# Graph-attention layer on 8192 nodes: the order of the first loads and of the first eight strips

## What is computed

```
in_fts = context @ W_common.T
left   = in_fts @ w_left + b_left
right  = in_fts @ w_right + b_right
logits = left[:, None] + right[None, :]
logits = where(logits >= 0, logits, 0.2 * logits)
logits = where(adj <= 0, -inf, logits)
y      = relu(softmax(logits, axis=-1) @ x)
out    = layernorm(x + y)
```

## Time and profile before

| | us |
|---|---|
| median of 3 runs | 1482.67 (1479.48 to 1483.78) |
| the profiled execution | 1482.25, of which its span 1480.4 |
| PE busy | 1375.9 (93% of the span) |
| DVE busy | 1306.0 (88%) |
| ACT busy | 643.1 (43%) |
| granted TensorE clock, mean | 0.965 |

### The profile page before, as it was taken

The page is one execution under the profiler, slowest core; times in us unless marked ns, Lnnn a source line. Parts: engine busy times, 40 slices in busy tenths (PEclk is TensorE's granted clock), DMA queues, the critical chain, the costliest instruction groups (busy, mean ns, idle before and its releaser), DMA issues.

```text
span 1480.4 us, 28323 instructions
## 1 busy us (share of the span) xinstructions
PE 1375.9 (93%) x12334; PEld 1207.8 (82%) x12334; DVE 1306.0 (88%) x1156; ACT 643.1 (43%) x675; POOL 72.6 (5%) x207
## 2 busy tenths in 40 slices
PE   1038999999999999999999999999999999999998
PEld 0014888888888888888888888888888888888887
DVE  6879999898989989898999989898998989899981
ACT  0187444444434444444435444444444444344441
POOL 0003000000000000000000000000000000000000
PEclk7558999999999999999999999999999999999999
DMA  9995998889899898989899898898989898988860
GB/s 378 314 283 127 232 235 226 228 213 230 221 229 233 217 225 214 238 207 242 217 231 223 215 234 215 225 224 234 229 214 232 207 238 213 236 221 220 208 169 9
DMA packets 82448, 329.59 MB, mean 223 GB/s; under 512 B 19728, under 2 KB 36112, under 8 KB 48528
## 3 DMA queue, kind: packets, MB, share of 16 engines
q1 hardware_dynamic: 79728, 321.47, 84.6%
q10 hardware_dynamic: 2592, 6.29, 1.4%
HBM read 319.29 MB, written 8.39 MB: 221 GB/s over the span
## 4 chain that ended last, share of the span: by engine, by line
PE 89%; SPq 5%; DVE 3%; ACT 2%; DMA 1%; issue 0%; POOL 0%; POOLq 0%; DVEq 0%
PE ps L351 30%; PE ps L354 29%; PE ps L353 29%; SPq L212 3%; DMA T<-in_x_dram 1%; DVE strip L671 1%; ACT X L399 1%; DVE T L715 1%; SPq L207 1%; SPq L235 1%; DVE X L620 0%; ACT X L394 0%; PE pt L325 0%; DVE xs L507 0%; ACT strip L428 0%
## 5 line engine op out<-in xcount | busy, mean ns | idle before, releaser
L351 PE MATMUL ps<-X,T 128*128 128x257 f16 x4096 | 1123.2, 274 | 7.1 <-ACT X L399 4.8
L354 PE MATMUL ps<-X,T 128*128 128x257 f16 x4096 | 1122.8, 274 | 0.0
L353 PE MATMUL ps<-X,T 128*128 128x257 f16 x4032 | 1101.3, 273 | 0.0
L428 ACT ACTIVATE strip<-strip 128x2048 f32<-128x2048 f32 x256 | 489.0, 1911 | 499.5 <-DMA strip<-in_adj_dram 490.1
L671 DVE SCALAR_TENSOR_TENSOR strip<-tab,arow,strip 128x2048 f32<-128x2048 f32 x256 | 598.0, 2336 | 56.8 <-ACT strip L428 56.0
L715 DVE STREAM_TRANSPOSE T<-strip 128x2048 f32<-128x2048 f32 x256 | 589.7, 2304 | 59.3 <-PE ps L354 59.2
L351 PEld LDWEIGHTS ps<-X,T 128*128 128x128 f16 x4096 | 403.0, 98 | 70.4 <-ACT X L399 15.5
L354 PEld LDWEIGHTS ps<-X,T 128*128 128x128 f16 x4096 | 402.5, 98 | 50.1
L353 PEld LDWEIGHTS ps<-X,T 128*128 128x128 f16 x4032 | 394.7, 98 | 48.9
L409 ACT ACTIVATE xs<-ps,small 128x256 f32<-128x256 f32 x64 | 30.4, 474 | 142.4 <-DVE small L720 142.4
L306 POOL TENSOR_SCALAR small<-small 128x1 f32<-128x1 f32 x64 | 12.3, 191 | 1270.5 <-ACT xs L417 1270.5
(11 more groups left out here) (90 smaller groups left out, 214.8 us busy)
## 6 DMA issues: line engine op xcount, KB each, us to landing
strip<-in_adj_dram SPq DMA_DIRECT2D x1016, 256.0 KB, 4.7
xs<-in_L_gnn_context_dram SPq DMA_DIRECT2D x14, 1024.0 KB, 9.9
T<-in_L_gnn_context_dram SPq DMA_DIRECT2D x4, 2048.0 KB, 17.6
X<-in_L_gnn_context_dram SPq DMA_DIRECT2D x4, 2048.0 KB, 34.1
xs<-in_x_dram SPq DMA_DIRECT2D x64, 128.0 KB, 5.2
out_dram<-xs SPq DMA_DIRECT2D x64, 128.0 KB, 5.1
gw<-in_L_gnn_context_dram SPq DMA_DIRECT2D x2, 1024.0 KB, 20.5
xs<-in_x_dram SPq DMA_DIRECT2D x4, 512.0 KB, 36.7
```

Of the source, the lines that this page charges most:

```text
L351: nc.tensor.matmul(ps[o][:, 0:D + 1], hi, X16[:, jb, 0:D + 1], start=(i == 0), stop=False)
L353: nc.tensor.matmul(ps[o][:, 0:D + 1], hi, X16[:, jb, XL:XL + D + 1], start=False, stop=False)
L354: m = nc.tensor.matmul(ps[o][:, 0:D + 1], lo, X16[:, jb, 0:D + 1], start=False, stop=(g > 0 and i == JB - 1))
L428: nc.scalar.activation(s, s, ACT.Relu, scale=KEEP).then_inc(s_m, 1)
```

## The change

Five edits, all to the order of the first eight strips.

1. Only strips 0 and 1 are loaded ahead of `x`; strips 2 and 3 are loaded behind it, on both queues.
2. ACT: `keep(0)` and `keep(1)` come first, then the issues of the last three chunks of `x` with the square sums of a chunk between them, then the issues for strips 2 and 3, then the last two chunks' square sums. `keep(2)` and `keep(3)` now come behind the high parts: 32 high parts, `keep(2)`, 6, `keep(3)`, 6, `keep(4)`, 7, `keep(5)`, 7, `keep(6)`, 6, `keep(7)`.
3. DVE: masks and transposes strips 0 and 1, makes `Fx`, makes 32 low parts, masks and transposes strips 2 to 7, and makes the other 20 low parts behind strip 7.
4. The order of the blocks is 63 to 32, 11 to 0, 31 to 12; POOL starts after 32 low parts.
5. PE: group 0 as 32 blocks' high products, their low products, the other high products and POOL's twelve low ones; then, once strip 7 is transposed, 20 whole blocks of group 1; then the last 20 low products of group 0; then the rest of group 1. Products and their number are the same.

```diff
+    NE = 2
-        order = list(range(JB - 1, -1, -1))
+        order = list(range(JB - 1, HB - 1, -1)) + list(range(NPL - 1, -1, -1)) + list(range(HB - 1, NPL - 1, -1))
+        PL = HB + NPL
+        R1 = 20
-        cut = [0, 44, JB - NPL, JB]
+        cut = [0, HB, HB + 6, HB + 12, HB + 19, HB + 26, JB]
...
             sp.wait_ge(s_v, 2)
-            for n in range(NB):
+            for n in range(NE):
                 for q in (0, 1):
                     strip_quarter(sp, n, q)
             sp.wait_ge(s_dot, 2 * CT)
             for c in range(NX):
                 for q in (0, 1):
                     x_quarter(sp, c, q)
+            for n in range(NE, NB):
+                for q in (0, 1):
+                    strip_quarter(sp, n, q)
...
-            pool.wait_ge(s_xl, JB - NPL)
+            pool.wait_ge(s_xl, HB)
...
+            pe.wait_ge(s_t, SG)
+            for i in range(HB):
+                high_products(0, i, i == 0)
+            for i in range(HB):
+                low_product(0, i)
+            for i in range(HB, JB):
+                high_products(0, i)
+            for i in range(HB, PL):
+                low_product(0, i)
+            pe.wait_ge(s_t, 2 * SG)
+            for i in range(R1):
+                high_products(1, i, i == 0)
+                low_product(1, i)
+            for i in range(PL, JB):
+                m = low_product(0, i, i == JB - 1)
+            m.then_inc(s_mm, 1)
+            for i in range(R1, JB):
+                high_products(1, i)
+                m = low_product(1, i, i == JB - 1)
+            m.then_inc(s_mm, 1)
...
-                rest_of_x(1)
-                rest_of_x(2)
                 keep(0)
                 keep(1)
-                rest_of_x(3)
-                rest_of_x(4)
-                keep(2)
-                keep(3)
-                for c in range(NX):
+                for c in range(2, NX):
+                    rest_of_x(c)
+                    square_sums(c - 2)
+                rest_of_first_group()
+                for c in range(NX - 2, NX):
                     square_sums(c)
-                for n in range(NB, NS):
+                for n in range(NE, NS):
...
-                    if n < SG - 1:
+                    if n + 1 < NE:
                         masked(n + 1)
-                    if n == SG:
+                    if n == NE:
                         x_factors()
                         dve.wait_ge(s_Fx, 1)
-                        for j in order[cut[0]:cut[1]]:
+                        for j in order[0:HB]:
                             low_part(j)
                         masked(n)
-                        for j in order[cut[1]:cut[2]]:
+                        dve.wait_ge(s_xl, HB)
+                    transposed(n, n % NB, g, g % 2, k)
+                    if n == 2 * SG - 1:
+                        for j in order[PL:JB]:
                             low_part(j)
                         dve.wait_ge(s_xl, JB - NPL)
-                    transposed(n, n % NB, g, g % 2, k)
-                    if SG <= n < 2 * SG:
+                    if NE <= n < 2 * SG:
                         masked(n + 1)
```

More of the change, by code:

```diff
@@ L341, in _, with high_products, low_product @@
             pe.wait_ge(s_one_col, 2)
-            for g in range(NG):
+            def high_products(g, i, first=False):
+                jb = order[i]
+                pe.wait_ge(s_xh, i + 1)
+                nc.tensor.matmul(ps[g][:, 0:D + 1], T16[:, g, jb, :, 1], X16[:, jb, 0:D + 1], start=first, stop=False)
+                nc.tensor.matmul(ps[g][:, 0:D + 1], T16[:, g, jb, :, 0], X16[:, jb, 0:D + 1], start=False, stop=False)
+            def low_product(g, i, last=False):
+                jb = order[i]
+                if HB <= i < PL:
+                    pe.wait_ge(s_xp, NPL - jb)
+                else:
+                    pe.wait_ge(s_xl, lows[i] + 1)
+                return nc.tensor.matmul(ps[g][:, 0:D + 1], T16[:, g, jb, :, 1], X16[:, jb, XL:XL + D + 1], start=False,
+                                        stop=last)
@@ L343, in _ @@
+            m.then_inc(s_mm, 1)
[3 more added lines that the diff above has]
+            m.then_inc(s_mm, 1)
+            for g in range(2, NG):
                 o = g % 2
                 pe.wait_ge(s_t, (g + 1) * SG)
-                if g >= 2:
-                    pe.wait_ge(s_y, g - 1)
-                for i, jb in enumerate(order if g == 0 else range(JB)):
+                pe.wait_ge(s_y, g - 1)
+                for jb in range(JB):
@@ L348, in _ @@
                     hi, lo = T16[:, o, jb, :, 1], T16[:, o, jb, :, 0]
[L349 to L355, removed]
@@ L356, in _ @@
-                    if i == JB // 4 and g % LB == 2 and g // LB + 1 < NLB:
-                        spread_left(g // LB + 1)
[L358 to L365, removed]
+                    nc.tensor.matmul(ps[o][:, 0:D + 1], hi, X16[:, jb, 0:D + 1], start=(jb == 0), stop=False)
@@ L366, in _ @@
+                    nc.tensor.matmul(ps[o][:, 0:D + 1], hi, X16[:, jb, XL:XL + D + 1], start=False, stop=False)
+                    m = nc.tensor.matmul(ps[o][:, 0:D + 1], lo, X16[:, jb, 0:D + 1], start=False, stop=(jb == JB - 1))
+                    if jb == JB // 4 and g % LB == 2 and g // LB + 1 < NLB:
+                        spread_left(g // LB + 1)
                 m.then_inc(s_mm, 1)
@@ L373, in _ @@
             act.wait_ge(s_v, 2)
-            for n in range(NB):
+            for n in range(NE):
                 for q in (2, 3):
                     strip_quarter(nc.scalar, n, q)
-            for c in range(1):
+            for c in range(2):
                 for q in (2, 3):
@@ L389, in rest_of_x, with rest_of_first_group @@
                     x_quarter(nc.scalar, c, q)
+            def rest_of_first_group():
+                for n in range(NE, NB):
+                    for q in (2, 3):
+                        strip_quarter(nc.scalar, n, q)
             def square_sums(c):
@@ L476, in _ @@
             with act.Else():
-                for c in range(1, NX):
+                for c in range(2, NX):
                     rest_of_x(c)
+                rest_of_first_group()
                 for c in range(NX):
@@ L775, in _ @@
                 dve.wait_ge(s_Fx, 1)
-                for j in order[0:JB - NPL]:
+                for j in order[0:HB] + order[PL:JB]:
                     low_part(j)
```

5 lines of the change are left out of this document (3 added, 2 removed).

## The result

The changed kernel takes 1484.73 us (median of 19 runs) beside 1480.69 for the kernel before (20 runs): a ratio of 1.0024, with a 95% interval of 1.0016 to 1.0031. A twentieth run of the changed kernel, at a granted clock of 0.55 where the others had 0.96, took 2503 us and is left out here and in all comparisons. The difference is 3.6 us by the ratio and 4.0 by the medians, slower by less than the 0.3% that I called no change. The forecast was +3.4 us.

The account below looks back on a forecast made before the run. Up to group 2 the load of x, then DVE's work behind the scale factors, were taken as the bound; PE after. Group 2 later, +1.3, plus clock, +2.1, gave +3.4 us, 1486.0; 8-in-10 range 1482.5 to 1489.5.

Parts of the forecast that it names:

- x earlier: Load of x: two strips, 2.1 MB, no longer ahead of it, so it lands 8.0 us earlier, bounds 6.0 and 9.0.
- A: The moment ACT starts its first high part: 98.44 us in the profile before, forecast 90.4 after the change.
- the 88 that I had set as the limit: Sign on the load of x: the forecast is wrong if x lands before 83 or after 88 us.
- DVE's extra work: DVE masks and transposes strips 2 and 3 behind the scale factors, 4.58 us a strip, 9.2 us more.
- The steps from A: DVE's path from ACT's first high part to strip 11's transposition: group 2 starts 73.5 us behind, at 163.9, +1.3 us.
- The thin cover of ACT's masks: Strips 2 to 7: ACT's masks stay 0.4 to 0.9 us ahead of DVE; each 0.1 us short costs that much.
- The clock: PE idles 4.4 us before group 2, then runs at half clock: +2.1 us, bounds 1.3 and 2.8.
- A (overtaking, +7.3): Rival: strips 2 and 3 on SP's queue overtake ACT's last quarters of x, which gains only about 4 us; chance 0.12.
- B: Rival: DVE is held by a late mask or group 0's products ending late, 1 to 3 us, 1487 to 1489; chance 0.10.
- C: Rival: PE's 4.4 us of idleness cost nothing or little, 1483.9 to 1484.5; chance 0.13.
- D: Rival: DVE's path is shorter than read, group 2 starts when PE allows, without idle, -3.2 us, 1479.5; chance 0.05.
- step 4: PE in groups 0 and 1: its later start is covered, group 1 being done 4.4 us ahead of strip 11.

Follow-up runs that it names:

- SP waits: The changed kernel, but SP issues its quarters of strips 2 and 3 only once the last chunk of x has landed; 1484.15 us, ratio 1.0026.
- both wait: The changed kernel with SP's strips 2 and 3 held until x has landed and ACT's issued behind its last square sum; 1483.77 us, ratio 1.0013.
- issues first: The changed kernel, but ACT issues all its x and strips 2 and 3 ahead of its first mask, square sums behind; 1486.52 us, ratio 1.0043.
- fed gap: The changed kernel with 36 extra matmuls, their results overwritten, on PE between groups 1 and 2; 1483.40 us, ratio 1.0013.
- groups in turn: The changed kernel without PE's interleaving: group 0 is finished before group 1 starts; 1483.60 us, ratio 1.002.
- 24 on POOL: The changed kernel with POOL making 24 low parts instead of 12 and PE finishing group 0 before group 1; 1477.84 us, ratio 0.9983.

## Why the prediction was right

The time was forecast as +3.4 us and came as +3.6 to 4.0; the mechanism was DVE's longer path against the earlier x, with a clock loss, and the profile shows each.

1. **x earlier** is the term that was mis-sized: 8.0 us forecast, 6.2 in the profiled pair (A at 92.27, not 90.4; the last square sum at 87.73, just inside the 88 that I had set as the limit). That is near the lower bound of 6.0, the bytes at x's own rate. The step priced x as a whole, and its upper bound took the two queues to run evenly. They did not: SP's last quarter of x landed at 82.3, 11.6 us earlier than before, ACT's at 87.7, only 2.0 earlier than the 89.7 of the lines below, and the later one counts. (An even end would have been near 85, an estimate from these landings, and would have gained 8.9 us.) The slow end of x, 232 GB/s from 80 to 90 us after 365 in the middle, is not new: the kernel before has 278 and 238 from 86 to 96. How much of ACT's delay is overtaking by SP's strips and how much its later issue stays open; holding the strips won back 0.1 to 1.6 us in timed runs. Nor is 6.2 firm: where the loads are the same, A is 91.18 to 92.80 in four profiles, and 98.44 and 98.97 in two with the order of before, a gain of 5.6 to 7.8; and if DVE's 9.3 and the clock's 1.7 hold in the timed runs, their +3.6 to 4.0 leaves 7.0 to 7.4 for it.

ACT's last quarter of x in the kernel before:

```profile
L212 ACTq DMA_DIRECT2D T<-in_x_dram x1: 4106/4106/4106, 71.2 to 71.2; - x1
DMA to landing us min/median/max: 18.5/18.5/18.5
```

2. **DVE's extra work**: 9.2 us forecast; group 2 moved from A+64.2 to A+73.5, 9.3.
3. **The steps from A** held to 0.2 us: first matmul of PE at A+24.15 (24.0), strip 7 transposed at A+42.4 (42.2), 20 low parts in 7.96 us (8.1), group 2 at A+73.47 (73.5). The three kernels that change only x's part (SP waits, both wait, issues first) have A+73.48 or A+73.49. The thin cover of ACT's masks held.
4. **PE**: done with group 1 at A+69.0 (69), idle 4.5 us (4.4). Strip 8's transposition was not held (its cover was put at 1.0 us).
5. **The clock**: 2.1 forecast, 1.7 in the profile, between the bounds of 1.3 and 2.8; shown by the fed gap, which gives it back.

In the profiled pair the terms that were off offset each other only in part (1.8 too little gain, 0.4 too much clock, 0.1 too little of DVE's work): it differs by 4.8 us, not 3.4. The timed runs put it lower, since the profiled execution of the changed kernel is itself 2.3 us above its median and that of the kernel before 1.6 above its own median of 20. That the number came so close is in part luck: the size of the gain of x is known no better than to 1 to 2 us.

Of the rivals, A (overtaking, +7.3) did not come in its size: the gain of x was 6.2, not 4, and removing all strips that could overtake brings 1 to 2 us at most. But its first half is seen in the profile, with ACT's last quarter landing 5.4 us behind SP's, and 6.2 is below the 6.9 at which it was to decide; only the timed runs, at +3.6 to 4.0, stay under the 4.4 us. B's held strip did not come. C falls with the fed gap: the clock's price is there. D did not come either. Group 2 can indeed start at A+68.8 with no idle of PE, and the time is then 1477.84, but only after 4.8 us of DVE's path have been taken away.

What I did not foresee is step 4's other side. I called PE's earlier order covered. It is, for group 2's start, yet the interleaving of groups 0 and 1 costs the clock's 1.7 us in the profile (1.1 by the medians, which do not establish it), because it makes the idle stretch fall where the clock counts.

## What to carry over

Count the critical engine's work from the moment at which the shared input is ready: moving work of that engine from its idle time before that moment to behind it costs its full length, and the load that comes forward must bring more than that. When TensorE will have to wait anyway, let it wait early, in its own slack, and arrive at the long stretch busy. When two queues share a load, look at where each of them ends: the later one counts. Before giving work to POOL, see what DVE does at the same time; and believe the medians of ten runs, not the profile of one, when the question is 2 us.

## What the runs showed of the hardware

- **The gate.** Idle stretches of 4.4 to 7 us before group 2 were followed by the half level of the clock (0.50 to 0.52 of 2.4 GHz, 1.2 GHz) and cost 1.6 to 3.0 us of the following stretch (1313.0 to 1314.4 against 1311.4); an idle of 1.15 us behind the fed gap cost nothing. The price did not follow the length of the idle: 4.4 us cost 3.0 in one kernel, 4.5 us cost 1.7 in another, 7.0 us cost 2.4. A long idle stretch is not needed: with the groups in turn the half level came behind nine waits of 0.3 us each (142.2 to 145.4, 16 matmuls).

- **DVE beside POOL.** A low part on DVE (scalar_tensor_tensor, 128x256) that starts while POOL runs a tensor_tensor lasts up to 2.36 us instead of 0.47. Both its inputs, `xs` and `X`, lie in SBUF, the on-chip memory that POOL's instructions read too. The page "SBUF — State Buffer" of the Trainium skill says in its section "SBUF: two separate sides" that a DVE instruction with two inputs in SBUF and a GpSimd instruction that reads SBUF exclude each other for a whole instruction, and that the one that starts first goes first; an extra of 1.9 us beside POOL instructions of 1.9 to 2.1 agrees. The masks of DVE have two tensor inputs as well, but only `strip` is in SBUF: `tab` is in PSUM, the memory of PE's results. They ran beside POOL at their usual length, six in the version with 24 on POOL at 2308 to 2350 ns, which agrees with the same rule:

```profile
L701 DVE SCALAR_TENSOR_TENSOR strip<-tab,arow,strip x6: 2308/2308/2350, 105.9 to 128.9; 128x2048 f32<-128x2048 f32 x6
```

- **Scatter of the loads.** A differs by 1.6 us between four profiled executions (one of each of four kernels) whose loads are the same (91.18 to 92.80). The three profiles in which SP's strips wait for x lie below all of these (88.16 to 89.81), and yet their timed runs gain 1.6 us at most. When x lands can't be told to 2 us from one execution.
